# One block for the three stages of an attention and mixture-of-experts layer, with steps reordered at both stage boundaries

## The reference, cut to what matters

```python
# _L0_attn_ref(x, ...), 16 heads, causal, on x of (4, 1024, 256)
q = x @ Wqa @ Wqb                      # per head 128 nope + 64 rope columns
ckv = x @ Wkva                         # 64 latent columns + 64 rope columns, shared by the heads
q_pe = _rope(q_pe);  k_pe = _rope(k_pe)
scores = jnp.einsum('bhnd,bhmd->bhnm', qf, kf) * scale
attn = jax.nn.softmax(jnp.where(causal, scores, min), axis=-1)
out = jnp.einsum('bhnm,bhmd->bhnd', attn, v);  return out @ Wout
# _L0_ffn_ref(x, ...), 64 experts in 8 groups, top 8
scores = jax.nn.softmax(x @ gate_w.T, axis=-1);  topk_w, topk_idx = jax.lax.top_k(scores, TOP_K)
flat = w_e[:, inv_map];  scalar = flat.sum(-1)
soft = jax.nn.softmax(jnp.where(flat == 0, NEG_INF, flat), axis=-1)
xg = x[:, None, :] + jnp.einsum('ngi,ghi->ngh', soft, mask_up_w)
a = jax.nn.silu(g) * u;  d = jnp.einsum('ngi,ghi->ngh', a, down_proj_w)
y = jnp.einsum('ng,ngh->nh', scalar, d)
# whole
x = x + _L0_attn_ref(_layernorm(x), ...);  x = x + _L0_ffn_ref(_layernorm(x), ...)
```

## Time and profile before

| what | value |
|---|---|
| median of 3 runs | 1628.61 us (1626.12 to 1631.35) |
| the profiled execution | 1630.55 us |
| its span | 1628.8 us, 68019 instructions |
| TensorE busy | 1538.3 us, 94% |
| VectorE, GpSimd, ScalarE busy | 71%, 57%, 49% |
| preparation | until about 73.5 us |
| attention, with the last body | 73.6 to 1158.6 us |
| FFN | 1159 us to the end |

### The profile page before, as it was taken

One profiled execution on the slowest core, in us unless ns is written; L12 is line 12 of the kernel. 1 busy time (PEld: TensorE's weight loads), 2 busy tenths in 40 slices (PEclk: granted clock), 3 DMA queues, 4 the chain that ended last, 5 costly groups with the idle time before them and its releaser, 6 DMA issues. The chain is left out here.

```text
span 1628.8 us, 68019 instructions
## 1 busy us (share of the span) xinstructions
PE 1538.3 (94%) x29426; PEld 1283.5 (79%) x29426; DVE 1157.9 (71%) x2607; ACT 800.5 (49%) x1725; POOL 933.3 (57%) x787
## 2 busy tenths in 40 slices
PE   5889999999999999999999999997799999999998
PEld 4668787877778877777778778886688888888887
DVE  6868887888788778877788778878555455445442
ACT  5655555555556555555555555553333333333332
POOL 3666767766767766767666667774342442342322
PEclk9989999999999999999999999999899999999999
DMA  7442221112331112222112221112521222123020
GB/s 261 147 108 74 49 55 46 52 42 74 78 78 49 49 52 78 61 68 62 56 49 67 65 58 53 37 35 87 147 66 53 78 72 79 46 72 88 24 85 13
DMA packets 98744, 114.72 MB, mean 70 GB/s; under 512 B 37456, under 2 KB 61776, under 8 KB 98448
## 3 DMA queue, kind: packets, MB, share of 16 engines
q1 hardware_dynamic: 98448, 110.39, 24.0%
HBM read 78.74 MB, written 15.07 MB: 58 GB/s over the span
## 5 line engine op out<-in xcount | busy, mean ns | idle before, releaser
L1571 ACT ACTIVATE probs<-aps,nmax 128x896 f32<-128x896 f32 (+7 forms) x512 | 378.1, 740 | 413.3 <-DVE nmax L1619 401.7
L1619 DVE CUSTOM_DVE_ANT_0 aps<-aps,mask_row 128x896 f32<-128x896 f32 (+7 forms) x512 | 380.8, 759 | 127.5 <-PE aps L47 123.9
L1297 POOL TENSOR_TENSOR rot<-rot,sinT 64x512 f32<-64x512 f32 x126 | 160.3, 1272 | 289.1 <-DMA rot<-rot 289.1
L47 PE MATMUL aps<-kTh,qh 128*128 128x512 f32 (+3 forms) x768 | 291.0, 379 | 9.2 <-ACT probs L1571 4.2
L47 PE MATMUL aps<-pT_second,vrep 32*64 32x128 f32 (+1 forms) x15616 | 264.5, 261 | 24.5 <-issue 21.9
L2041 POOL TENSOR_TENSOR sg<-sg,mass_b 128x512 f32<-128x512 f32 x88 | 114.7, 1303 | 291.2 <-ACT sg L1939 290.8
L47 PEld LDWEIGHTS aps<-pT_second,vrep 32*64 32x64 f32 x15616 | 225.9, 131 | 64.1 <-issue 51.6
L1629 DVE STREAM_TRANSPOSE pT_second<-probs 128x896 f32<-128x896 f32 (+3 forms) x256 | 264.2, 1033 | 6.0 <-ACT probs L1571 5.9
L47 PE MATMUL aps<-kTl,qh 128*128 128x512 f32 (+3 forms) x768 | 259.9, 346 | 1.1 <-issue 1.1
L1987 DVE TENSOR_TENSOR act_sb<-fps,sg 128x512 f32<-128x512 f32 x88 | 60.6, 689 | 230.3 <-PE fps L47 179.6
L47 PE MATMUL aps<-kTh,ql 128*128 128x512 f32 (+3 forms) x768 | 222.6, 344 | 0.0
(11 more groups left out here) (205 smaller groups left out, 2917.2 us busy)
## 6 DMA issues: line engine op xcount, KB each, us to landing
linv_b<-inverses_scratch SPq DMA_DIRECT2D x128, 128.0 KB, 3.0
mass_b<-mass_scratch SPq DMA_DIRECT2D x64, 256.0 KB, 4.0
rot<-rot SPq DMA_DIRECT2D x252, 64.0 KB, 2.5
wqs<-wq_scratch SPq DMA_DIRECT2D x30, 256.0 KB, 3.7
mass_b<-mass_scratch SPq DMA_DIRECT2D x48, 96.0 KB, 3.9
raw_numbers<-in_x SPq DMA_DIRECT2D x8, 512.0 KB, 6.2
vrep<-values_scratch SPq DMA_DIRECT2D x16, 256.0 KB, 4.4
inverses_scratch<-linv_t SPq DMA_DIRECT2D x256, 1.0 KB
```

The lines of the kernel that those rows point to most:

```text
L47: return nc.tensor.matmul(out, lhsT, rhs, start=start, stop=stop, skip_group_check=True)
L1297: eng.tensor_tensor(rot2[:, k, :], rot2[:, k, :], t.sinT[:, cols], ALU.mult).then_inc(q_turned, 1)
L1571: nc.scalar.activation(probs[:, SLOT[x, r], 0:w], sps[:, at:at + w], ACT.Exp, bias=nmax[:, c, a, j:j + 1], scale=-1.0, accum_out=lsum[:, c ...
L1619: nc.vector.tensor_tensor_reduce(out=s, in0=s, in1=mask[:, N - PW[c][j]:N], scale=-1.0, scalar=3.0e38, op0=ALU.add, op1=ALU.min, accum_out ...
```

## The change

All three stages stand in one block. The barriers between them are gone, and what they ensured is now said with waits: TensorE waits before bodies 0 and 8 for keys and queries (`keys_made`, `first_queries`) and for each bank's last reader in the stage before (`bank_free`); the other engines wait for the last piece of a kind (`last_of`). The eight banks of the second and third stage are one tensor. The first stage gets a buffer of its own for rotated keys.

In body 0, `ROT(1, 1)` moves from GpSimd to VectorE, behind the third maximum, and banks are given out anew. SyncE no longer waits for the stores of `wq` before it stores the values.

In the last body, `R(3)` stands before PV(1,5) and `R(4)` before PV(1,6), `R(7)` moves from the next stage into this one, ScalarE's `R(4)` ahead of `OHIGH(1)`, `ZERO` ahead of `OLOW(1)`, and the products of n = 0 (`F(0)`, `F(1)`) stand between MASK and the last `Y`. `MASK` no longer waits for `O(1)`. In the next stage router part 5 comes first on TensorE and on ScalarE; ScalarE's four weight pieces are cut in two pairs, behind part 5 and behind part 6, with the first SiLU behind them; it waits for the x2 stores before the first high part of the down weights. SyncE issues the last x2 stores after the spread of the mass of blocks 0 to 3.

```diff
-        sp.wait_ge(wq_stored, 16 * (PAIRS - 2))
...
-        VECTOR_FIRST = [MAX(0, 1, 1), MAX(0, 1, 3), MAX(0, 0, 1), MAX(0, 1, 0), TURN(0, 1, 1), MAX(0, 0, 3),
+        VECTOR_FIRST = [MAX(0, 1, 1), MAX(0, 1, 3), MAX(0, 0, 1), ROT(1, 1), MAX(0, 1, 0), TURN(0, 1, 1), MAX(0, 0, 3),
...
-        TENSOR_LAST = [R(0), R(1), PV(1, 0), R(2), Y(0, 0), Y(0, 1)] + [PV(1, n) for n in range(1, PARTS[1])] + \
-            [R(3), R(4), MASK, Y(1, 0), Y(1, 1)]
+        TENSOR_LAST = [R(0), R(1), PV(1, 0), R(2), Y(0, 0), Y(0, 1), PV(1, 1), PV(1, 2), PV(1, 3), PV(1, 4), R(3),
+                       PV(1, 5), R(4), PV(1, 6), PV(1, 7), MASK, F(0), F(1), Y(1, 0), Y(1, 1)]
...
-                       O(1), R(6), MASK, ACC(1, 0), ACC(1, 1)]
-        SCALAR_LAST = [R(0), R(1), QUAD(0), QUAD(2), QUAD(1), R(2), R(3), OHIGH(1), MASK, R(4)]
-        POOL_LAST = [STATS, OLOW(1), ZERO]
+                       R(6), O(1), R(7), MASK, ACC(1, 0), ACC(1, 1)]
+        SCALAR_LAST = [R(0), R(1), QUAD(0), QUAD(2), QUAD(1), R(2), R(3), R(4), OHIGH(1), MASK]
+        POOL_LAST = [STATS, ZERO, OLOW(1)]
...
+            for kind in ("proj_ps", "u_low", "x_normal", "scale_ready", "prod_low", "rope_low"):
+                sp.wait_ge(*t.last_of[kind])
...
-            all_added(LAST - 1)
-            for n in range(4):
-                store_acc(B - 1, n)
+
+            def finish():
+                all_added(LAST - 1)
+                for n in range(4):
+                    store_acc(B - 1, n)
...
+                    for bank in banks_of(x, r):
+                        if USERS[bank][0] == (x, r):
+                            for reader in t.bank_free[bank]:
+                                pe.wait_ge(*reader)
...
+                    if pair in (0, PAIRS):
+                        for made in t.keys_made[b]:
+                            pe.wait_ge(*made)
...
-                    pe.wait_ge(o_sb, count(O(1), r))
                     mask_products(nc, t, 0, banks[:, BANK_LAST[MASK], :])
...
+                def first_job(x):
+                    banks_free(x)
+                    pe.wait_ge(t.first_low, len(PIECES[0]))
+                    pe.wait_ge(t.xT_l, 2)
+                    expert_products(nc, t, banks[:, bank_of(x, r), :], 0, x[1], slice(0, HN))
...
+            act.wait_ge(*t.last_of["prod_ps"])
...
+                    if r == 0 and c == 1:
+                        dve.wait_ge(t.wq_stored, 16 * (PAIRS - 2))
...
             sp.wait_ge(t.mass_kept, 64)
+            sp.wait_ge(*t.values_read)
             for m in range(4):
                 spread_mass(0, m)
+            t.finish_attention()
             load(2)
...
-                    for k in (0, 1):
-                        products(0, k)
+                    pe.wait_ge(*t.o_read)
+                    router_tensor(nc, t, 0, 5, r_bank)
+                    pe.wait_ge(t.mw_l, 1)
                     products(1, 0)
-                    router_tensor(nc, t, 0, 5, r_bank)
+                    for u in range(2):
+                        soft(0, u)
+                    pe.wait_ge(t.fl_sub, 1)
                     products(1, 1)
...
-            second_quad_high()
             router_scalar(nc, t, 0, 5, r_bank)
+            second_quad_high(SECOND_QUAD[0:2])
             router_scalar(nc, t, 0, 6, r_bank)
+            second_quad_high(SECOND_QUAD[2:4])
             for n in range(TOTAL):
                 silu(n)
                 if n == 0:
+                    act.wait_ge(t.x2_stored, 64 * B)
                     down_high(0)
...
+        with ExitStack() as sems, nc.Block() as block:
+            t.sem = lambda name: sems.enter_context(nc.semaphore(name))
```

149 lines of the change are left out of this document (89 added, 60 removed).

## The result

The changed kernel takes 1619.78 us (median of 4 runs, 1617.84 to 1621.22) against 1628.5 us for the kernel before: a ratio of 0.9944 with a 95% interval of 0.9926 to 0.9963, 8.7 us faster. On a second chip the ratio was 0.9954 (0.9937 to 0.9971). The forecast of 1625.1 us had the sign and the range (1618.5 to 1629.5) right, but the gain is two and a half times the 3.5 us of its sum; the nearest of the cases was the first rival, at 1620.3, though the gain came by other pieces than that rival's.

A forecast was written before the change was run, and what follows sets the result against it. TensorE was taken to set the pace in attention and the last stage. First boundary -1.3, attention bodies +0.8 and last boundary -3.0 sum to -3.5 us, from 1628.61 to 1625.1 us; range 1618.5 to 1629.5.

The forecast's parts named there:

- the first rival: Last body: third instruction block arrives ahead of the down weights, clock stays up; 1620.3 us in all; chance 0.25.
- First boundary: Preparation to attention: TensorE starts 3.2 us sooner, but Q(0,0) gains only 1.3 us, bounds -0.3 to 2.
- Attention bodies: Attention stage: same work, but 90 more waiting TensorE instructions shift the block boundaries; +0.8 us, with 3 us allowed.
- Last body: Last attention body, walked block by block from PV(1,1) at 1132.27: three stops, value pieces ending at 1148.0.
- T0: End of the last body's value pieces; forecast 1148.0 us, bounds 1145 and 1149.2.
- the first stop: Last body, soon after PV(1,1): TensorE still stops for instructions, its next block coming at 1137.4.
- The third block: Last body: instruction block asked for at 1141.2, as the down weights are issued; taken to come at 1147.2.
- A third stop of under 1 us: Last body: a third instruction stop this short was listed as showing the forecast wrong.
- Last boundary: Attention to last stage: TensorE's second product of block 2 at T0 + 19.1; gain 3.0 us, bounds 1.8 and 7.1.
- A fetch at each branch from scratch: Both stage boundaries: TensorE fetches the branch target's block anew, 3.5 us each; 1632.1 us; chance 0.07.
- The wait that changes its place at the first swap: First boundary: swap late behind the value store, VectorE held; third block takes 7.0 us; 1627.6 us; chance 0.15.
- Nine more stops: Block boundaries shifted by 86 instructions make 9 more of them stop TensorE, 1.0 us each; 1634 us; chance 0.05.

The follow-up runs named there:

- e1: The changed kernel run again with nothing altered; 1615.76 us against 1623.26 before.
- e6: Changed kernel with 170 waiting TensorE instructions spread over bodies 1 to 7, so 256-instruction blocks fall as in the kernel before from body 8; 1623.34 us, ratio 0.998.
- e7: Changed kernel with the second half of the expert weights issued later, just in front of the down weights; 1615.63 us, ratio 0.9941.
- e8: Changed kernel with waiting TensorE instructions filling each body to 7 times 256, one or two ahead of each long product; 1636.12 us, ratio 1.0067.
- e9: Changed kernel with the first rope step, ROT(1,1) of body 0, back on GpSimd; 1612.46 us, ratio 0.9936.
- e4: Changed kernel with 3584 waiting TensorE instructions, in rows ahead of five groups per body, filling each body to 7 times 256; 1905.66 us.
- e2: Kernel before with 86 waiting TensorE instructions in two rows (46, 40), so 256-instruction blocks fall as in the changed kernel; 1623.57 us, ratio 1.0003.
- e3: Changed kernel with 170 waiting TensorE instructions in a row in body 0, so blocks fall as in the kernel before from body 8; 1630.97 us, ratio 1.005.
- e5: Kernel before with 86 waiting TensorE instructions spread over bodies 0 and 8, two or three per product group; 1627.24 against 1627.19 us, ratio 1.0003.

## Why the prediction was right, and where it was off

The time lay in the range, and part of that is luck: of the three terms of the sum the middle one was wrong by more than its bounds, and the last one was right by other stops than those told.

**First boundary: right.** Forecast 1.3 us at Q(0,0), measured 1.7 (2.92 less the 1.25 of the early clock), or 1.5 counted from the last transposes; in four more traces with this order (e1, e6, e7, e8) it is the same 12.9 us from there. Add these 1.25 us to the changed kernel's rows and they stand beside the forecast: the first maximum at 72.13 (forecast 72.25), the rope from 75.63 to 77.63 (75.4 to 77.4), Q(0,0) at 82.40 (82.7). That a start 3.2 us sooner would turn into a wait was the point, and it did: 5.88 us. The step didn't ask what the rope on VectorE itself is worth, since it came in one package with the barrier; e9 says it costs 1.0 us there.

**Attention bodies: the wrong term.** It was +0.8 us from an average over the blocks, with 3 us to either side. Measured from Q(0,0) to PV(1,1) it is -2.95, outside these bounds: -3.98 until body 2 and +1.03 behind it. What is behind can't be told from chance, since the same program differs there by 6.6 us (e1). For bodies 0 and 1 the average hid two stops that the trace before had shown, each with a half clock behind it. The windows of the kernel before around them (us, busy of the five engines, clock, DMA share, GB/s), at 1.2 GHz for most of both; its stops were 1.57 us at 101.05 and 2.03 at 110.24:

```profile
101.00:105.00 4.00, 3.95 (x13) 3.40 (x14) 2.28 (x4) 2.19 (x6) 1.67 (x2) 0.57 0.01 2
111.00:115.00 4.00, 4.00 (x73) 3.63 (x81) 2.23 (x8) 1.00 (x4) 3.92 (x4) 0.59 0.01 4
```

And the changed kernel over the same work:

```profile
86.00:120.00 34.00, 31.46 (x870) 25.52 (x868) 27.93 (x59) 20.26 (x47) 26.35 (x21) 1.00 0.33 88
```

There is no stop of over 0.2 us for instructions, and the clock is full. The last body had been walked block by block; bodies 0 and 1, where 46 of the 86 instructions are added, should have been too. Until the last few microseconds TensorE, once up, ran at half clock for 41 us before and for 20.5 us in the changed kernel's trace; in the other traces of this study, e4 left out, it was 14 to 38 us. (The price of a stop that a rival uses, 27.4 us for 28 stops, is a little high too: the 28 sum up to 25.4 us, 0.9 each.)

**Last body: the sum right, by other stops, which is luck.** With 5.9 us for the common start taken out, T0 was 1147.0 (1141.1 + 5.87); the forecast said 1148.0 within 1145 to 1149.2. Of its steps, the first stop did not remain: the packet for the next block but one had started at 1124.61, 1.8 us before PV(1,1), while TensorE was still at R(2) and the output products, so two blocks were there. The forecast had a block asked for on entering the one before it, and this packet came ahead of that. "R(3) follows (its input is ready by then)" was false, it waited 2.27 us for VectorE. And the block whose turn came at 1128.24, under the expert weights, gave the 2.48 us. The third block slipped in: its packet started at 1136.40, 1.0 us behind the issue of the down weights, and there was no stop. A third stop of under 1 us was on the forecast's own list of what would show it wrong. It is also half of the first rival, which had 0.25; its time for the request (1141.2, measured 1141.22 with 5.87 added) came out exact, though the first of the two stops ahead of it was not there. The rival's 1620.3 us is near the measured 1619.8 by luck: it had 7.1 us at the last boundary, where 3.5 were measured, and nothing in bodies 0 and 1, where 4.0 were.

**Last boundary: right.** TensorE's second product of block 2 was forecast at T0 + 19.1 and came at 1141.1 + 19.1; the first weighing ended 18.2 us behind T0 (forecast 18.4). The clock fell in the wait of 2.81 us as feared and cost 1.57 us (10.90 to 9.33) where 1.0 was charged. In all 3.46 us for 3.0. But what earned them is another matter: the forecast told them as the fruit of the earlier products and the missing barrier, and e2, e3, e5 and e6 give most of them to the cut. The 3.32 us of the barrier were not won; they came back as waits of 1.74 and 2.81 us and as half clock. The two chips show 7 to 9 us. The traces place some 1.5 of them at the first boundary, 3 to 4 in bodies 0 and 1 and 3.5 at the end; the first of these, and at most 1.1 us of the last, is owed to what the change set out to do.

**Rivals.** A fetch at each branch from scratch: out, the first query product starts 0.64 us behind the transposes of the other stage, as fast as the eight of them run. The wait that changes its place at the first swap: out, the rope started where it was forecast. Nine more stops: out, 34 waits for issue instead of 33. Of the totals that the forecast named, the 24 to 31 us of waits for issue fit the first trace (24.9) and not the second (17.0).

## What to carry to other kernels

- Where TensorE runs thousands of short products, look at the packets of its instruction queue beside its timeline. Nearly every stop for "issue" of 0.3 us or more lies at a multiple of 256 instructions from the others (27 of 28 in the kernel before); an edit anywhere ahead of it, even a few waits, moves it, and the gain of an edit is only known against the same cut.
- Keep large loads away from stretches that use up instructions fast. One moved line gave the kernel before 6 us in its last body and 5.2 up to the first down product, more than all the reordering at that boundary; in the whole time it is 3.7 us (0.3 to 7).
- When a step goes to a faster engine, ask what stands behind it in that engine's queue: the move of the rope cost 1.0 us, and letting the ready maxima pass ahead of it gave back 1.2.

## What the runs showed of the hardware that was not expected

- A wait on TensorE that is already satisfied costs 0.09 to 0.1 us when many stand in a row (3.62 us for 40 in e2, 17.0 for 170 in e3), and next to nothing (at most 0.4 us for 117, e8) when one or two stand ahead of each long product.
- TensorE goes on 2.2 to 3.4 us (2.4 in the middle) after the start of the packet it stopped for, over 295 stops of 0.3 us or more in thirteen traces, e4 left out. When the packet itself starts is less regular. From the entry into the block before, it took 0.8 to 1.7 us for half of the blocks (1.1 in the middle), and 2.2 in the middle at the stops. In 3 to 4% the packet came before the entry. A large transfer makes it late (4.7 us, and 0.9 with the transfer moved, e7), but it isn't the only reason: ahead of the stop at 110.24 in the kernel before it came 6.3 us after the entry with the DMA engines 5% busy, and behind 683.51 in the changed kernel 5.25 us after it with no other packet moving. Why is open.
- The Trainium skill (Runtime: NRT & Kernel Launch, Instruction fetch mechanics) gives the same blocks of 256 and calls the cost of a crossing mostly hidden. Here most crossings are hidden (28 of 205 in the attention stage of the kernel before stopped TensorE for 0.3 us or more), but the others add up to waits for issue of 17 to 27 us in that stage.
- The same program differs by 6.6 us in the attention stage from one execution to the next, and its waits for issue by 8 us (e1).
